# Attention's outputs kept turned: packed by DMA, divided on GpSimd instead of VectorE

## The reference, cut to what matters

```
for each batch b, key-value head kv, query head j of its four:
    P = exp(scores - row maximum), 0 for keys behind the query      # 1024 x 1024
    O[b, :, head] = (P @ V) / sum(P)                                 # 1024 x 16
x = x + O.reshape(tokens, 256) @ Wout + bout
xn = layernorm(x); logits = xn @ gate_w                              # for the last layer
```

## Time and profile before

| what | value |
|---|---|
| median of three runs | 2545.34 us (2545.29 to 2553.23) |
| profiled execution, own time | 2548.63 us |
| its span | 2546.9 us |
| mean granted TensorE clock | 0.948 |
| TensorE (matmul) busy | 2258.4 us, 89% of the span |
| VectorE busy | 1786.6 us, 70% |
| ScalarE busy | 1339.8 us, 53% |
| GpSimd busy | 1340.4 us, 53% |
| attention's steady part, per unit | 29.3 us |

### The profile page before, as it was taken

How to read it: one execution, slowest core, us unless ns; L and a number is a source line. 1 busy time by engine, 2 the same in 40 slices (tenths; PEclk the granted TensorE clock), 3 DMA queues, 4 the chain that set the end, 5 groups by cost and what they waited for, 6 DMA issues and landing times. The chain is left out here.

```text
span 2546.9 us, 34973 instructions
## 1 busy us (share of the span) xinstructions
PE 2258.4 (89%) x11358; PEld 1329.1 (52%) x11359; DVE 1786.6 (70%) x2734; ACT 1339.8 (53%) x2581; POOL 1340.4 (53%) x1024
## 2 busy tenths in 40 slices
PE   8895888989988988599986699999998569999998
PEld 3342444544544545599973334444444336666666
DVE  6998999999999997655557899999993651111100
ACT  5777887787788786322224456666665311111110
POOL 1545999899899895377755312222222123334332
PEclk9997999999999999799997789999998779999999
DMA  5457245125125112644437612222200503333322
GB/s 165 150 186 260 102 131 194 37 77 185 42 77 180 50 50 85 190 71 72 72 60 165 144 33 34 34 42 42 34 3 4 199 25 83 66 71 70 74 50 25
DMA packets 149681, 231.36 MB, mean 91 GB/s; under 512 B 26257, under 2 KB 98769, under 8 KB 149394
## 3 DMA queue, kind: packets, MB, share of 16 engines
q1 hardware_dynamic: 120258, 190.44, 24.8%
q0 software_dynamic: 29280, 39.11, 9.5%
HBM read 152.43 MB, written 81.66 MB: 92 GB/s over the span
## 5 line engine op out<-in xcount | busy, mean ns | idle before, releaser
L1263 POOL TENSOR_TENSOR scan_hC<-scan_h,scan_c_all 128x1024 f32<-128x1024 f32 x256 | 612.5, 2416 | 65.0 <-DVE scan_h L1118 63.8
L1118 DVE TENSOR_TENSOR_SCAN scan_h<-scan_dA,banks 128x1024 f32<-128x1024 f32 x224 | 504.5, 2275 | 21.3 <-ACT scan_dA L1040 12.9
L893 PE MATMUL banks<-scan_hC,all_ident 128*128 128x512 f32 x1024 | 486.9, 600 | 26.4 <-DVE scan_xc L1125 26.4
L2346 ACT ACTIVATE attn_pt<-banks 128x1024 f32<-128x1024 f32 (+3 forms) x384 | 292.3, 810 | 183.1 <-PE banks L2293 180.2
L1033 ACT ACTIVATE scan_scaled<-mamba_duT,mamba_bT 128x128 f32<-128x128 f32 x1024 | 312.0, 388 | 20.5 <-PE banks L870 20.1
L2230 POOL TENSOR_SCALAR_AFFINE_SELECT attn_pt<-attn_pt 128x256 f32<-128x256 f32 x256 | 102.6, 407 | 376.7 <-ACT attn_pt L2346 375.0
L893 PEld LDWEIGHTS banks<-scan_hC,all_ident 128*128 128x128 f32 x1024 | 185.3, 191 | 179.3 <-issue 129.2
L3084 DVE TENSOR_TENSOR ffn_y<-banks,ffn_gates 128x512 f32<-128x512 f32 x32 | 22.1, 691 | 334.7 <-PE banks L2842 328.0
L3131 POOL DMA_INDIRECT out<-ffn_y,ffn_ids x64 | 105.3, 1645 | 270.5 <-DVE ffn_y L3084 260.8
L2368 DVE TENSOR_REDUCE attn_m_lo<-banks 128x1 f32<-128x512 f32 (+3 forms) x368 | 225.9, 657 | 26.3 <-PE banks L2249 20.0
L2249 PE MATMUL banks<-attn_K,attn_Q 96*128 96x512 bf16 (+3 forms) x768 | 230.9, 340 | 7.1 <-DVE attn_mask L2358 5.9
(11 more groups left out here) (354 smaller groups left out, 3873.5 us busy)
## 6 DMA issues: line engine op xcount, KB each, us to landing
scan_c_all<-scratch_bc SPq DMA_DIRECT2D x64, 512.0 KB, 5.8
ffn_w<-in_e_w SPq DMA_DIRECT2D x16, 1024.0 KB, 5.4
attn_Q<-scratch_q SPq DMA_DIRECT2D x96, 128.0 KB, 4.1
scratch_x<-front_xc SPq DMA_DIRECT2D x8, 1024.0 KB, 5.8
scratch_z<-front_zs SPq DMA_DIRECT2D x8, 1024.0 KB, 7.5
scan_xc<-scratch_x SPq DMA_DIRECT2D x16, 512.0 KB, 3.6
scan_zs<-scratch_z SPq DMA_DIRECT2D x16, 512.0 KB, 4.6
scratch_dt<-front_lw SPq DMA_DIRECT2D x7, 1024.0 KB, 4.1
```

The source lines that it names most:

```text
L893: mm = pe.matmul(PS[:, YB + i, :], ident[:, :], hC[:, u % NHC, i * BANK:(i + 1) * BANK], start=s == 0, stop=s == NST - 1, skip_group_check ...
L1118: dve.tensor_tensor_scan(h[:, u % NH, :], decay, drive, 0.0, ALU.mult, ALU.add).then_inc(scanned, 1)
L1263: pool.tensor_tensor(hC[:, u % NHC, :], h[:, u % NH, :], c_all[:, s, :], ALU.mult).then_inc(hC_done, 1)
L2346: act.activation(pt[:, at % 4, 2 * pair:2 * pair + 2, 0:width], PS[:, ST + 2 * pair:ST + 2 * pair + 2, 0:width], ACT.Exp, scale=HD ** -0.5 ...
```

## The change

`o_turn`, `turn_out`, `divide_out`, `o_all`, `turn_o`, `copy_oT` and `oT` go. The outputs keep channels on the partitions, which is the layout that the projection's stationary operand needs. A new class `HeadOutputs` holds what replaces them. For unit w: SP sends all of `ot` and, again, its four rows of sums to DRAM (`send`); reads the 4,096 sums back as 128 partitions of 32 (`take_sums`); VectorE inverts them in place (`invert`); SP puts the inverses to DRAM (`put_inverses`), and takes, head by head, 16 partitions of outputs into `dense` and the head's inverses, repeated over 16 partitions, into `spread` (`take`, eight transfers); GpSimd multiplies 64 partitions by 1,024 (`scale`). The steps of a unit are spread over the next three. ScalarE's `copy_out` of unit w waits for the sends of unit w-1 in place of the reciprocal. Of the last three units the rest is done in `project_scores`: SP's part ahead of its row writes, two inverts on VectorE at t = 1 and 7, and three scales at the head of GpSimd's program. `project(t)` waits at t = 0, 8, 16, 24 for the scales of that batch, and the wait for the gate's load moves behind the tiles.

```diff
-SHARES = (3, 3, 5, 2, 3, 5, 4, 4, 5, 3, 3, 2)
+SHARES = (3, 3, 4, 2, 3, 4, 4, 4, 5, 3, 3, 2)
...
-    events.insert(16, ("o_turn", w, 0))
-    events.insert(18, ("m_turn", w + 1, 0))
+    events.insert(17, ("m_turn", w + 1, 0))
     events.insert(1, ("m_turn", w, 1))
-    events.insert(6, ("o_turn", w - 1, 1) if w else None)
...
+class HeadOutputs:
+    def by_lane(self, rows):
+        return rows.rearrange("j (c x) -> (j c) x", x=GH * SEQ // P)
+
+    def send(self, sp, w):
+        sp.wait_ge(self.copied, 2 * w + 2)
+        sp.dma_start(self.dram[w, :, :], self.ot[:, :]).then_inc(self.put, 16)
+        sp.dma_start(self.sums_dram[w, :, :], self.ot[HD:P:VW, :]).then_inc(self.put, 16)
+
+    def take_sums(self, sp, w):
+        sp.wait_ge(self.put, 32 * (w + 1))
+        if w >= 2:
+            sp.wait_ge(self.inv_put, 16 * (w - 1))
+        sp.dma_start(self.sums[:, w % 2, :], self.by_lane(self.sums_dram[w, :, :])).then_inc(self.sums_in[w % 2], 16)
+
+    def invert(self, dve, w):
+        dve.wait_ge(self.sums_in[w % 2], 16 * (w // 2 + 1))
+        dve.reciprocal(self.sums[:, w % 2, :], self.sums[:, w % 2, :]).then_inc(self.inverted, 1)
+
+    def put_inverses(self, sp, w):
+        sp.wait_ge(self.inverted, w + 1)
+        sp.dma_start(self.by_lane(self.inv_dram[w, :, :]), self.sums[:, w % 2, :]).then_inc(self.inv_put, 16)
+
+    def take(self, sp, w):
+        b, kv = divmod(w, NKV)
+        sp.wait_ge(self.inv_put, 16 * (w + 1))
+        if w >= 2:
+            sp.wait_ge(self.scaled, w - 1)
+        for j in range(GH):
+            first = kv % 2 * GH * HD + j * HD
+            to = slice(first, first + HD)
+            sp.dma_start(self.dense[to, kv // 2, b * SEQ:(b + 1) * SEQ], self.dram[w, j * VW:j * VW + HD, :]
+                         ).then_inc(self.taken[w % 2], 16)
+            sp.dma_start(self.spread[to, :], self.inv_dram[w, j:j + 1, :].to_broadcast([HD, SEQ])).then_inc(self.taken[w % 2], 16)
+
+    def scale(self, pool, w):
+        ...
+        pool.wait_ge(self.taken[w % 2], 16 * 2 * GH * (w // 2 + 1))
+        pool.tensor_tensor(own, own, self.spread[rows, :], ALU.mult).then_inc(self.scaled, 1)
+        pool.wait_ge(self.scaled, w + 1)
...
             for w in range(NU):
                 send_maxima(w, 1)
+                if w:
+                    outs.send(sp, w - 1)
                 if w + NKV - 1 < NU:
...
                     load_heads(sp, heads, q_dram, k_dram, w + NKV - 1)
                 if w + 1 < NU:
                     send_maxima(w + 1, 0)
+                if w:
+                    outs.take_sums(sp, w - 1)
+                if w >= 2:
+                    outs.put_inverses(sp, w - 2)
+                    outs.take(sp, w - 2)
...
+                    if x == HK and w >= 3:
+                        pool.wait_ge(future_cut, cuts_through(w, x))
+                        outs.scale(pool, w - 3)
...
                 if w:
-                    act.wait_ge(o_step, 2 * w + h - 1)
+                    act.wait_ge(outs.put, 32 * w)
...
+                    if x == HK and w >= 2:
+                        outs.invert(dve, w - 2)
...
             for loads in ahead:
                 loads.start(sp)
+            outs.send(sp, NU - 1)
+            outs.put_inverses(sp, NU - 2)
+            outs.take_sums(sp, NU - 1)
+            outs.take(sp, NU - 2)
+            outs.put_inverses(sp, NU - 1)
+            outs.take(sp, NU - 1)
...
             def project(t):
-                pe.wait_ge(oT_copied, t + 1)
+                if t % TPB == 0:
+                    pe.wait_ge(outs.scaled, NKV * (t // TPB + 1))
...
-                    mm = pe.matmul(PS[:, OB + t % 2, 0:DM], oT[:, t % 2, c, :], w_out[:, c, :], start=c == 0, stop=c == KC - 1)
+                    mm = pe.matmul(PS[:, OB + t % 2, 0:DM], outs.dense[:, c, t * P:(t + 1) * P], w_out[:, c, :], start=c == 0, stop=c == KC - 1)
...
-            gate_loads.wait(pe)
-            turn_o(0)
             for t in range(NT):
-                if t + 1 < NT:
-                    turn_o(t + 1)
                 project(t)
                 if t in TURN_AT:
                     turn_xn(TURN_AT[t])
+            gate_loads.wait(pe)
...
+                if t in (1, 7):
+                    outs.invert(dve, NU - 2 + (t == 7))
...
+            for w in range(NU - 3, NU):
+                outs.scale(pool, w)
```

More of the change, by code:

```diff
@@ L2117, in unit_events @@
         mine = events[at:at + share]
-        out.append([[e for e in mine[share * i // SLOTS:share * (i + 1) // SLOTS] if e] for i in range(SLOTS)])
+        out.append([mine[share * i // SLOTS:share * (i + 1) // SLOTS] for i in range(SLOTS)])
         at += share
@@ L2127, in schedule, with __init__ @@
     fill = maxima_of(0, 0) + [("m_turn", 0, 0)] + maxima_of(0, 1)
-    ending = [("o_turn", NU - 1, 1)]
-    in_order = fill + [e for unit in units for step in unit for slot in step for e in slot] + ending
-    return fill, units, ending, {e: k for k, e in enumerate(in_order)}
+    in_order = fill + [e for unit in units for step in unit for slot in step for e in slot]
+    return fill, units, {e: k for k, e in enumerate(in_order)}
+class HeadOutputs:
+    def __init__(self, nc, n):
+        right = lambda name, shape: nc.alloc_sbuf_tensor(f"attn_{name}", shape, F32, side="right")
+        self.dense, self.ot, self.spread = right("o_dense", [P, KC, TOK]), right("ot", [P, SEQ]), right("spread", [P, SEQ])
+        self.sums = right("sums", [P, 2, GH * SEQ // P])
+        self.dram, self.sums_dram, self.inv_dram = scratch(nc, "o", [NU, P, SEQ]), scratch(nc, "sums", [NU, GH, SEQ]), scratch(nc, "inv", [NU, GH, SEQ])
+        self.copied, self.put, self.inverted, self.inv_put, self.scaled = (
+            n.sem(x) for x in ("ot_copied", "o_put", "inverted", "inv_put", "scaled"))
+        self.sums_in = [n.sem(f"sums_in{i}") for i in range(2)]
+        self.taken = [n.sem(f"o_taken{i}") for i in range(2)]
+    def by_lane(self, rows):
[27 more added lines that the diff above has]
+    def scale(self, pool, w):
+        b, kv = divmod(w, NKV)
+        rows = slice(kv % 2 * GH * HD, (kv % 2 + 1) * GH * HD)
+        own = self.dense[rows, kv // 2, b * SEQ:(b + 1) * SEQ]
+        pool.wait_ge(self.taken[w % 2], 16 * 2 * GH * (w // 2 + 1))
+        pool.tensor_tensor(own, own, self.spread[rows, :], ALU.mult).then_inc(self.scaled, 1)
+        pool.wait_ge(self.scaled, w + 1)
@@ L2151, in load_heads, with attention @@
                      ).then_inc(q_in[kv], 16)
[L2154 removed]
+def attention(nc, g, v_all, heads, outs, w_out, q_dram, k_dram, m_dram, out_sem, weights):
     with ExitStack() as ctx:
@@ L2262, in turn_maxima @@
                              ident[:, :]).then_inc(piece_made, 1)
[L2264 to L2267, removed]
-                    mm = pe.transpose(PS[:, k % NSB, i * P:(i + 1) * P], ot[:, at:at + P], ident[:, :])
-                mm.then_inc(piece_made, 1)
             def pieces(events):
@@ L2326, in _ @@
             weigh_v(NU - 1, NSTEP - 1)
-            pieces(ending)
         @block.scalar
@@ L2421, in _, with project_scores @@
                         pieces(slot)
-            pieces(ending)
-def project_scores(nc, g, o_all, w_out, xnT, xn_all, rows_to, gate, ahead):
+                    if x == HK and w >= 2:
+                        outs.invert(dve, w - 2)
+def project_scores(nc, g, outs, w_out, xnT, xn_all, rows_to, gate, ahead):
     with ExitStack() as ctx:
@@ L3273, in lists_layer @@
                 gate = gate_weights(nx, g["gate2"])
-                project_scores(nc, g, o_all, w_out, xnT, xn_all, xn_rows, gate, ahead=(gate[-1], consts[-1]))
+                project_scores(nc, g, outs, w_out, xnT, xn_all, xn_rows, gate, ahead=(gate[-1], consts[-1]))
             choose_experts(nc, g, lane, vals, xn_rows, out_rows, consts)
```

62 lines of the change are left out of this document (15 added, 47 removed).

## The result

The changed kernel took 2523.41 us (median of four runs, 2521.95 to 2524.78), the kernel before 2545.82 on the same chip: a ratio of 0.9901, 95% interval 0.9889 to 0.9913. That is 22.4 us faster. The forecast was 2518.6, range 2508 to 2534.

A forecast was written before the change was run, and what follows sets the result against it. TensorE was taken as full and VectorE nearly so in attention, TensorE as the limit behind it. Attention's 13.5 and the stage's 13.2 us sum to 26.7: 2521.9 profiled, 3.3 lower for the median, 2518.6, range 2508 to 2534.

The forecast's parts named there:

- 0.9, TensorE's share, since it is the fuller: Attention: each of units 1 to 14 shortens by 0.9 us, TensorE's part of the removed turns; 12.6 us.
- rival A: Attention: VectorE counts for more, its whole 0.7 us is gained in two steps a unit; total 33.7 us, 2511.6; chance 0.12.
- C: Attention gains nothing, since a loop through exponentials and banks sets the step; only 13.2 us gained, 2532.1; chance 0.06.
- (c): Attention: ScalarE's first copy now waits until both transfers of the previous unit's ot land; cost nothing.
- 2.1 us spare: Attention: both transfers land by about 1659.2, ScalarE's copy comes at 1661.3, so it has 2.1 us spare.
- edge of 6.6 us: Attention: transfers of ot up to 6.6 us stay covered, 1655.82 to 1662.4; beyond this each us costs one per unit.
- D: Attention: ScalarE's copy waits for the landing; 8.4 us transfers eat the 26.7 us gain, 9 us gives 2554.6; chance 0.07.
- E: Attention: ScalarE's copy waits for landings of 7.9 us, which eats 19.5 us: 2538.1, no change; chance 0.06.
- (d): Attention: SP's added issues, 5.4 us a unit, and a round trip make nothing late; 0, upper 1 us a unit.
- (e): Attention: GpSimd's 64x1024 multiply, 2.36 us, fits its 13 us gap and misses VectorE's invert; cost 0, bounds 0 to 2.4 a unit.
- rival B: GpSimd's multiply holds the invert 0.5 us a unit, last chain delays turn_xn by 5; total 14.7 us, 2530.6; chance 0.13.
- 1 us spare: Stage behind attention: GpSimd's normalise(1), behind scale(15), comes at 1962.5, turn_xn(0) near 1963.6; cost 0, bounds 0 and 5.

The follow-up runs named there:

- e1: Changed kernel with only TensorE's four transposes of each old o_turn put back, twice in each of 15 units: 2534.74 us, ratio 0.9949 to the kernel before.
- e2: Changed kernel with only VectorE's old division put back (reciprocal and product, twice a unit, result unused): 2530.72 us, ratio 0.9934 to the kernel before.
- e12: Changed kernel with GpSimd's normalise(1) and (3) ahead of scale(15), timed beside the unchanged one on the same chip: 2517.89 us, ratio 0.9886 to the kernel before.
- e3: Changed kernel with SP's two sends of ot behind the twelve head loads instead of ahead: 2618.36 us, ratio 1.0276 to the kernel before.
- e5: Changed kernel with VectorE's reciprocal of the sums one step earlier, beside GpSimd's multiply: 2522.20 us, ratio 0.9903 to the kernel before.
- e10: Changed kernel plus an unread two-input VectorE addition of 128x32 beside GpSimd's multiply, units 3 to 15: 2533.29 us, ratio 0.9941 to the kernel before.
- e6: Changed kernel with attention's multiply of 64x1024 on VectorE instead of GpSimd, units 3 to 15: 2528.77 us, ratio 0.9929 to the kernel before.
- e11: The changed kernel again, unchanged, for a second profile and more times: 2522.68 us, ratio 0.9900 to the kernel before.
- e9: Changed kernel with GpSimd's normalise(1) and (3) ahead of scale(15), first chip: 2519.42 us, ratio 0.9895 to the kernel before.
- e7: Changed kernel with unit 15's sends ahead of the five loads of the next layer's weights: 2521.14 us, ratio 0.9902 to the kernel before.
- e4: Changed kernel with the wait for the gate's load back ahead of the first projection: 2527.47 us, ratio 0.9916 to the kernel before.

## Why the prediction was right, step by step

**Attention, 13.5 us forecast: 14.2 by the marks.** The term "0.9, TensorE's share, since it is the fuller" is shown from both sides: e1 takes 0.92 a unit back with TensorE's part alone (+13.1), e2 0.3 with VectorE's. Together e1 and e2 give back 17.6, more than the 14.2, so the two costs don't simply add; how they overlap wasn't tried. And e2 put back 0.87 us of VectorE, less than the net 1.1 that the change took (26.78 to 25.7). Still, VectorE's relief, which rival A priced at 0.5 a unit on top, mostly lies in time that TensorE sets. A and C fall.

**(c) ScalarE's wait, cost nothing: right, with less to spare than forecast.** No copy waits in the changed kernel's profile. In most units the sums leave 3.65 us behind the second half's copy and the next copy comes at 8.74, so both transfers have 5.1 us from the sums' issue, 5.5 from the send's, as the forecast's 1655.82 to 1661.3. By the traces' semaphore events they were in 2.6 us behind the sums' issue in the median, 3.1 behind the send's, where the forecast had 3.4. But the slowest took 4.75, and in the unit shown above, with its long round trip, they were in at 1659.68, 0.09 ahead of the copy. In e12's profile one copy did wait, for sums issued at 1653.23:

```profile
1657.10 0.60 ACT L2384 ACTIVATE attn_ot<-banks 128x512 f32<-128x512 f32 x1 [0.18 <-DMA scratch_sums<-attn_ot]
```

So the "2.1 us spare" is right for the usual unit, and the forecast didn't see that a slow round trip takes it all. The edge of 6.6 us isn't borne out: it added ScalarE's idle 1.15 us to the 5.5, and e3 shows 0.3 of it hidden (5.17 against 4.87). The price of "each us costs one per unit" is too low as well: in e3 a wait of 5.9 us made the unit 7.8 longer. The forecast's time doesn't rest on either, but those of rivals D and E do. Neither rival came true: ahead of the loads in the queue both transfers were in 2.6 us behind the sums' issue in the median, where e3, behind them, has 4.8.

**(d) SP: right.** The next maxima write leaves at 1664.10, when cut. TensorE's weight loads wait for maxima coming back from DRAM twice, 0.8 us in all; before it was once, 0.3.

**(e) GpSimd's multiply, cost 0: right, for a reason I hadn't seen.** I counted on a miss "by a us"; they miss by 0.37, and e5 shows that a hit would cost nothing. The hold of rival B is real for e10's addition, with two inputs in SBUF: 1.29 us more in VectorE (1.465 against 0.171) cost 0.93 a unit in e10, about seven tenths, where e2 and e6 cost a third and a half. There the work was spread, or came once the multiply was gone; that the place makes this difference is argued, not shown.

**The stage, 37.9 us from 1941.6 forecast, 36.8 measured** (1929.97 to 1965.88, and 0.87 for the last tile). The terms, of which the first was the author's estimate, without a row; 27.7 is 32 tiles of 1.085 less 0.22, 5.3 is twelve turn_xn of 0.44 (1975.72 to 1977.24 less 1.085), and the clock's 2.5 was chosen below the 2.7 lost before from tile 0 to tile 3, in 5.97 us for 3 x 1.085:

| term | forecast | measured |
|---|---|---|
| start behind GpSimd's last addition | 0.45 | 0.36 |
| 32 tiles | 27.7 (0.865) | 27.8 (0.868) |
| turn_xn | 5.3 (12) | 4.8 (only 11 lie ahead of tile 31) |
| clock | 2.5 | 0 in this execution; some 1.6 in e11's |
| VectorE's pushes | 1.6 | 0.9 |
| root waits | 0.8 | 1.3 |
| GpSimd ahead of turn_xn(0) | 0 | 2.1, of which the wait is 1.85 |

Two terms were off and nearly cancelled. That is luck in part: in e11's profile, with a longer wait for GpSimd and the clock's fall behind it, the stage took 38.9, so that the forecast lies between the two executions. The clock: the forecast expected TensorE idle between the stages again, if for less, and the clock low behind it. It stood idle, for 1.26 us where the earlier trace rows had 3.75, and the clock stayed at 1.00. No run shows that the 2.5 must come with the pause: in e2 and e6 the clock fell behind 1.26 us, here it didn't. The other is the "1 us spare" ahead of turn_xn(0). Scale(15) was forecast to end 20.3 us behind the first projection (1961.9 less 1941.6) and did (1950.27 less 1929.97). TensorE was to want turn_xn(0) after 22.0 us (1963.6), and with no time lost to the clock was ready for it after 19.3 (1951.08, less the wait of 1.85, less 1929.97). So the spare us became a wait of two, which the forecast had named as a sign of being wrong. e9 and e12 show that the order on GpSimd makes it; e7 shows that SP's order at the stage's head doesn't take it away.

**The median, 4.8 us above the forecast.** The sum fitted the profiled executions to 0.1 us, which is luck: the changed stretches gained 28.6 in that profile, 2 more than forecast, and the part ahead of attention, which nobody changed, took 2.7 of it back. The medians differ by 22.4. The step that failed is "the median lies 3.3 lower, and so is the forecast": the profiled execution of the kernel before, 2548.63, lies 2.8 above its median, and that of the changed kernel is its shortest (2521.95 of 2521.95 to 2524.78). Part of the changed kernel's spread is shown: e11's profiled execution, 2523.98 us, lost 2.1 us against the first one from the first projection on: 0.5 in the wait for GpSimd, the rest behind it, with the clock at 0.50, while the first one kept 1.00. Of the seven profiles with this order on GpSimd in which TensorE waits ahead of turn_xn(0), the clock fell there in five (e1, e3, e5, e10, e11) and stayed in two (the first, e7). The part ahead of attention, the same code in all, varies too: the first maxima piece stands at 1449.2 to 1454.0 us in the thirteen profiles.

## What to carry to other kernels

Price a saving by the engine that is fuller, then ask what the slack of the other can hide: here TensorE's microsecond counted whole and VectorE's by a third where it was spread, by half to seven tenths where it came in one block. Before a GpSimd operation with two SBUF inputs is put beside VectorE, sort VectorE's instructions there by their inputs: here those with two inputs in SBUF stood until GpSimd was done (1.465 us for 0.171 in e10), while a reciprocal (0.35 for 0.34), statistics and additions out of a bank (0.42 either way), with one input in SBUF, passed. Other kinds with a single input have to be tried. When a stage gets shorter, look again at work that comes by DMA at a time of its own, and put what the fuller engine waits for ahead of it.

## What the runs showed of the hardware that was not expected

A VectorE addition of 128x32 with both inputs in SBUF lasted 1.465 us in the median beside GpSimd's multiply and 0.171 alone; a reciprocal of the same size in SBUF 0.35 beside it and 0.34 alone. e6's timeline has both sorts, of 128x16, within one multiply; alone the second took 0.17:

```profile
1952.95 2.34 POOL L2181 TENSOR_TENSOR attn_o_dense<-attn_o_dense,attn_spread 64x1024 f32<-64x1024 f32 x1 [4.50 <-DMA attn_spread<-scratch_inv]
1953.06 0.23 DVE L2646 RECIPROCAL oln_rstd<-oln_rstd 128x16 f32<-128x16 f32 x1
1953.33 2.00 DVE L2648 SCALAR_TENSOR_TENSOR oln_nmr<-oln_mean,oln_rstd 128x16 f32<-128x16 f32 x1
```

The granted clock was not the same after the same pause. With TensorE idle for 1.25 to 1.26 us ahead of the first projection, it stayed at 1.00 in the changed kernel (both profiles), e1, e3, e5, e7, e9, e10 and e12, and fell to 0.50 in e2 and e6; after e4's 3.12 us it fell too. Ahead of turn_xn(0) it stayed at waits of 1.61 and 1.85 us (e7, the changed kernel's first profile) and fell at 2.03, 2.32, 2.40, 2.52 and 2.53 (e5, e11, e1, e10, e3). But in e2 it stayed at 1.00 behind a pause of 2.03 us in the same stage (1952.89), so the pause's length alone doesn't decide. What tells e2 and e6 apart from the others at the stage's start isn't settled by these runs.

The same two transfers of an ot, 512 KB and its sums, were in 4.0 to 5.2 us after the sums' issue behind the twelve loads of the same queue (e3, twelve units, median 4.8); ahead of them, in the changed kernel's first profile, after 2.45 to 4.75 us, median 2.6 (fifteen units, by the semaphore events of the traces).
